# A two-layer transformer kernel without the constant products in TensorE's planned holes

## The reference, cut to what matters

```python
x = L0_attn_x                                     # (8, 1024, 256)
x = x + attn0(layernorm(x), w_qkv, w_out)         # 16 heads of 16, causal softmax
x = x + ffn0(layernorm(x), proj, C1, Win1, Wout1, C2, Win2, Wout2)
x = x + attn1(layernorm(x), Wq_down, ..., Wc)     # latent 64 per head, rotary half, causal
x = x + ffn1(layernorm(x), Ws1, Ws2, W1, W2, Wr)  # shared expert + top-2 of 8, prob truncated
# ffn0: a = entmax15(layernorm(x @ proj)); h = gelu(((x,1) @ Win1 * (a @ C1)) @ Wout1.T)
#       out = ((h,1) @ Win2 * (a @ C2)) @ Wout2.T
# ffn1: relu(x @ Ws1)**2 @ Ws2 + trunc(softmax(top2(x @ Wr))) * expert outputs
```

## Time and profile before

| | |
|---|---|
| runs, median (lowest to highest) | 2942.04 us (2939.97 to 2944.25) |
| the profiled execution's own time | 2941.76 us |
| its span, first to last instruction | 2940.0 us |
| mean granted TensorE clock | 0.975 of full |
| TensorE busy (its matmuls) | 2637.8 us, 90% |
| VectorE, ScalarE, GpSimd busy | 2091.0, 1895.6, 948.8 us |
| filler products, line 1119, busy (435 of 520 have a record) | 119.2 us |
| chain that ended last, by engine | PE 64%, ACT 13%, DVE 13%, issue 5% |

### The profile page before, as it was taken

The page is one execution under the profiler, slowest core; times in us unless marked ns, Lnnn a source line. Parts: engine busy times, 40 slices in busy tenths (PEclk is TensorE's granted clock), DMA queues, the critical chain, the costliest instruction groups (busy, mean ns, idle before and its releaser), DMA issues.

```text
span 2940.0 us, 56496 instructions
## 1 busy us (share of the span) xinstructions
PE 2637.8 (90%) x18768; PEld 1101.7 (37%) x18853; DVE 2091.0 (71%) x5808; ACT 1895.6 (64%) x3868; POOL 948.8 (32%) x1646
## 2 busy tenths in 40 slices
PE   6989998999889998999989999899988999889987
PEld 4334432334333443334433343333433334333432
DVE  4865687857868588685887668776687757878483
ACT  3565665767566766667666675576766776566655
POOL 2214241425214251243413234142521425114411
PEclk9999999999999999999999999999999999999999
DMA  5202120212102120121211112011210213101120
GB/s 185 55 1 60 44 55 18 68 47 80 37 27 64 57 80 18 32 75 45 75 26 42 56 58 69 19 58 42 77 49 24 62 46 89 31 25 46 32 59 16
DMA packets 138734, 150.43 MB, mean 51 GB/s; under 512 B 15920, under 2 KB 122832, under 8 KB 138448
## 3 DMA queue, kind: packets, MB, share of 16 engines
q1 hardware_dynamic: 138448, 146.74, 17.3%
HBM read 78.46 MB, written 67.11 MB: 50 GB/s over the span
## 4 chain that ended last, share of the span: by engine, by line
PE 64%; ACT 13%; DVE 13%; issue 5%; POOL 1%; DMA 1%; SPq 0%; ACTq 0%; DVEq 0%; POOLq 0%
PE ps L1254 15%; PE ps L1170 9%; ACT probs L1557 9%; PE ps L1235 7%; PE ps L1194 7%; PE ps L1162 6%; DVE mx L1824 4%; PE ps L1333 4%; PE ps L1328 4%; DVE ps L1821 4%; PE ps L1119 2%; PE ps L1320 2%; PE ps L1262 2%; PE ps L1208 1%; PE ps L1137 1%
## 5 line engine op out<-in xcount | busy, mean ns | idle before, releaser
L1557 ACT ACTIVATE probs<-ps 128x512 f32<-128x512 f32 (+2 forms) x2560 | 1235.0, 564 | 371.5 <-PE ps L1235 365.5
L1824 DVE TENSOR_REDUCE mx<-ps 128x1 f32<-128x512 f32 (+2 forms) x1536 | 900.3, 639 | 251.5 <-PE ps L1208 125.9
L1821 DVE CUSTOM_DVE_ANT_0 ps<-ps,mask_b 128x512 f32<-128x512 f32 (+1 forms) x1024 | 614.6, 650 | 251.4 <-PE ps L1194 249.6
L1729 POOL TENSOR_SCALAR_AFFINE_SELECT probs<-probs 128x256 f32<-128x256 f32 (+1 forms) x768 | 368.8, 484 | 1110.9 <-ACT probs L1557 1108.5
L1254 PE MATMUL ps<-probs,vaug 128*17 128x512 f32 (+3 forms) x6144 | 618.7, 513 | 8.7 <-ACT probs L1557 3.7
L1194 PE MATMUL ps<-stk_k,stk_q 48*128 48x512 f16 (+3 forms) x3072 | 458.3, 333 | 60.8 <-issue 36.6
L1235 PE MATMUL ps<-stk_q,stk_k 50*128 50x512 f16 (+3 forms) x3072 | 439.0, 333 | 63.5 <-ACT probs L1557 20.5
L1194 PEld LDWEIGHTS ps<-stk_k,stk_q 48*128 48x128 f16 x3072 | 138.1, 94 | 437.8 <-issue 347.3
L1235 PEld LDWEIGHTS ps<-stk_q,stk_k 50*128 50x128 f16 x3072 | 131.5, 94 | 440.8 <-issue 338.4
L1162 PE MATMUL ps<-turned,wqkv 128*128 128x512 f32 x512 | 262.0, 619 | 9.2 <-ACT scratch L1522 2.1
L1254 PEld LDWEIGHTS ps<-probs,vaug 128*17 128x17 f32 x6144 | 139.6, 98 | 295.9 <-issue 202.0
(11 more groups left out here) (171 smaller groups left out, 2902.0 us busy)
## 6 DMA issues: line engine op xcount, KB each, us to landing
stk_q<-q SPq DMA_DIRECT2D x256, 96.0 KB, 2.5
stk_k<-k SPq DMA_DIRECT2D x128, 192.0 KB, 3.6
q<-parts SPq DMA_DIRECT2D x64, 256.0 KB, 2.3
k<-parts SPq DMA_DIRECT2D x64, 256.0 KB, 2.2
stk_k<-k SPq DMA_DIRECT2D x128, 96.0 KB, 2.5
x<-in_L_attn_x SPq DMA_DIRECT2D x16, 512.0 KB, 4.0
q<-parts SPq DMA_DIRECT2D x64, 128.0 KB, 2.8
k<-parts SPq DMA_DIRECT2D x64, 128.0 KB, 2.1
```

Source lines behind the costliest of these rows:

```text
L1557: act.activation(probs[:, step % PBUF, heads, cols], src, ACT.Exp, scale=exponent[l])\
L1729: pool.affine_select(out=diag, in_=diag, compare_op=ALU.is_ge, fill=0.0, base=0, pattern=[[0, k], [1, P]], channel_multiplier=-1).then_inc ...
L1821: dve.tensor_tensor_reduce(tile, tile, mask_b[:, BANK - width:BANK], 1.0, LOWEST, ALU.add, ALU.max, most)\
L1824: dve.tensor_reduce(most, tile.rearrange("q (k w) -> q k w", k=k), AX.X, ALU.max)\
```

## The change

The products are no longer issued, and with them go the note in the planner, the two constants, the helper and its eight calls. The wait on `pool_chain` ahead of the first place goes too. `ORDER` stays as it is.

```diff
--- before.py
+++ after.py
@@ -649,9 +649,6 @@
         else:
             what()
         if what != "wait":
-            item = plan.order[made]
-            if gap > FILL_FROM and item[0] in ("xt", "yt", "at", "st", "mt", "s", "nm", "lg", "rt"):
-                FILL[item] = int(gap / FILL_TIME)
             gap = 0.0
 
     order = plan.order
@@ -682,8 +679,6 @@
 RANK = dict(mt=1, nm=2, burst=3, late=4, st=5, pair=5.5, due=6, s=7, chain=8, single=10)
 EARLY = True
 
-FILL_TIME, FILL_FROM = 0.25, 0.7
-FILL = {}
 
 PLACE = {}
 FINISH = []
@@ -1112,12 +1107,6 @@
                 return t_bank[b], full[b]
 
 
-            def keep_going(key, pt):
-                if FILL.get(key, 0) and key == next(iter(FILL)):
-                    pe.wait_ge(pool_chain, 9)
-                for _ in range(FILL.get(key, 0)):
-                    pe.matmul(pt, ident_b[:], mask_b[:], start=True, stop=True)
-
             def tile(key):
                 b = PLACE[key][0]
                 return t_bank[b], full[b]
@@ -1131,7 +1120,6 @@
 
             def transposed_x(n, b, c, kd):
                 pt, done = claim(("xt", n, b, c, kd))
-                keep_going(("xt", n, b, c, kd), pt)
                 pe.wait_ge(xn_ready, 2 * (LN["rstd", n, b, c] + 1))
                 for i in range(TPC):
                     ins = pe.transpose(pt[:, P * i:P * (i + 1)], xn[:, i, P * kd:P * (kd + 1)], ident[:])
@@ -1184,7 +1172,6 @@
                 c, slot = UNITS[u][3], u % NBUF
                 width = dict(score_parts(i))[p]
                 n, tiles = packed(width), [claim(("s", u, i, h, p, r)) for r in range(2)]
-                keep_going(("s", u, i, h, p), tiles[0][0])
                 pe.wait_ge(stk_loaded[slot], 16 * STACK_DMAS * (u // NBUF + 1))
                 for a in range(n):
                     for r in range(2):
@@ -1213,7 +1200,6 @@
 
             def max_rows(u):
                 pt, done = claim(("mt", u))
-                keep_going(("mt", u), pt)
                 rows = pt[0:2 * NP * PAIRS, 0:BANK // 2].bitcast(F16)
                 pe.wait_ge(mx_ready, u + 1)
                 for i in range(TPC):
@@ -1223,7 +1209,6 @@
             def scores_t(u, j, h):
                 c, slot = UNITS[u][3], u % NBUF
                 tiles = [claim(("st", u, j, h, r)) for r in range(2)]
-                keep_going(("st", u, j, h), tiles[0][0])
                 if j == 0 and h == 0:
                     pe.wait_ge(m_loaded, 16 * MAX_DMAS * (MT["mt", u] + 1))
                 a, z = query_range(j, c)
@@ -1264,7 +1249,6 @@
 
             def transposed_y(b, l, c, kd):
                 pt, done = claim(("yt", b, l, c, kd))
-                keep_going(("yt", b, l, c, kd), pt)
                 in_sbuf(pe, ("nm", LAST_UNIT[b, l, c]))
                 for i in range(TPC):
                     ins = pe.transpose(pt[:, P * i:P * (i + 1)], y[:, PASS[b, l, c] % 2, i, P * kd:P * (kd + 1)], ident[:])
@@ -1285,7 +1269,6 @@
 
             def narrow_product(key, n, b, c, w):
                 pt, done = claim(key)
-                keep_going(key, pt)
                 need_xT(n, b, c)
                 for kd in range(KD):
                     for t in range(TPC):
@@ -1300,7 +1283,6 @@
 
             def transposed_a(b, c):
                 pt, done = claim(("at", b, c))
-                keep_going(("at", b, c), pt)
                 pe.wait_ge(a_ready, ENT["epow", b, c] + 1)
                 for i in range(TPC):
                     ins = pe.transpose(pt[0:STRIP + E0, P * i:P * (i + 1)], zu[:, i, :], ident[:])
```

## The result

| | median | lowest to highest | runs |
|---|---|---|---|
| before | 2940.39 us | 2934.94 to 2950.33 | 18 |
| changed | 2948.9 us | 2940.61 to 2958.18 | 18 |

The account below looks back on a forecast made before the run. TensorE's fillers were taken to be partly on the path, standing behind bank waits and starving ScalarE. 2941.8 - 45 (path) + 25 (clock falls) + 6.5 (covered phases, tail, start) gave 2928 us, range 2898 to 2958 us.

Parts of the forecast that it names:

- The gain on the path (45 us): Time returned at the end by dropping fillers: at most 60 us from 278 on the path, taken as 45 us.
- the place of rows 4: Three fillers behind a bank's wait, ahead of a score product: ScalarE's idle 0.89 us would shrink to 0.24 us.
- rival B: TensorE would wait for VectorE, ScalarE or a DMA instead: 30 us gained, 25 + 6.5 lost, 2943 us; chance 0.18.
- The 90 places: Places of the 278 fillers taken to be on the path, each 0.216 us, 60 us in all if fully returned.
- 23 falls: New drops to the lower clock between 90 and 2780 us, 3.3 us long, 1.1 us lost each: 25 us.
- The sevens: Six runs of seven fillers ahead of `s` items, beside the maxima's DMAs: 42 fillers, removal gives 0.
- eight thin stretches a batch: 5 us stretches with TensorE too little busy once fillers go; three in eight lose the clock, 3 new falls a batch.
- the 33 places: Places of the 242 fillers taken to be covered by VectorE, a DMA or other waits: removal gives 0 path.
- the three covered phases: 68 to 90, 255 to 283, 2780 to 2829 us: clock falls almost surely, only the way back up costs, 3 us.
- the tail: Last transpositions and products after 27 fillers and 3 behind: no path gain, 3 us lost at the lower clock.
- Rival A: Holes between 90 and 2780 us stay thin, 45 falls at 1.3 us: +20 us, 2961 us; decides from 35 falls; chance 0.24.
- Rival C: Fillers never bought clock between 90 and 2780 us; only tail and edges are lost: 2903 us; chance 0.15.

Follow-up runs that it names:

- the first experiment: From the kernel before, keeps only the 242 fillers at 33 places taken as covered and drops the 278 at the other 90: 2917.67 us, ratio 0.9919.
- experiments 9 and 10: From the kernel before, 95 fillers ahead of `st` items dropped (9): 2927.74 us, 0.9951; 165 ahead of `s` items dropped (10): 2923.39 us, 0.9937.
- experiment 2: From the kernel before, keeps the 278 fillers at 90 places and drops the 242 at the 33 covered places: 2969.36 us, ratio 1.0091.
- experiment 5: The changed kernel with only the six runs of seven fillers (42, ahead of `s` items) put back: 2926.66 us, ratio 0.9956 to the kernel before.

## Why the prediction was wrong

**The gain on the path (45 us).** The mechanism was right: the place of rows 4 gives 0.67 us, the seven lay beside the DMA. Subtracting the starts of the same ScalarE instructions in the kernel before and in the first experiment's, the batch from 1392 to 1744 us has seven steps clear of a fall, of 0.25 to 0.79 us, together 4.4 us; others lie beside a difference in clock. The five batches of both have 89 us at the lower level, so that their 18.4 us are path alone: 3.7 a batch, where 5.9 were forecast. For the whole program, the 24 us of the first experiment and what its clock lost make 33 us by the profiled execution and up to 40 us by the runs' medians. 45 was too high; that of a filler's 0.216 us only 0.11 to 0.15 reach the end (experiments 9 and 10) is in line with rival B's mechanism, other waits that follow.

**The 90 places as a whole.** The prediction had 23 falls for all places between 90 and 2780 us. The sevens were one of its eight thin stretches a batch, at three in eight, so six of them were some 2 falls, and the 90 places had -45 + 21 x 1.1 = -22 us; the first experiment measured -24 us. Its clock says 6 falls more by the profiled execution and 13 by the runs' medians, not 21. The sum is right, and its two terms are each too large: that is luck. (The eight doesn't follow from the rule beside it either. Twelve places a batch, one a seven and half of the other eleven thin, are 6.5 stretches; that would have been 19 falls, 20 us and a forecast of 2923 us.)

**The step that failed: the price of the covered places.** For the 33 places at which removal gives no path, the prediction had some 2.5 us for the six sevens (2 falls), about one price each for the three covered phases (3 us), 3 us for the tail and 0.5 for the start: 9 us. They cost 31 us (2948.9 against 2917.67), and 28 us when they alone were dropped (experiment 2). The reasoning was that VectorE or a DMA covers what happens there, and that a hole brings down the clock for one fall or none. The first is so in the place itself: from 68.6 to 90.1 us the changed kernel ran at

```profile
68.60:90.10 21.50, 11.82 (x77) 5.42 (x76) 20.02 (x66) 3.62 (x7) 2.56 (x8) 0.63 0.08 24
```

and VectorE is as busy as in rows 7. But the lower level outlasts the hole and meets work that has no cover. Its longest stretch, in the place of unit 8's 34 fillers, has the length of seven falls, where one price was taken:

```profile
258.30:282.30 24.00, 12.47 (x77) 6.86 (x79) 17.09 (x74) 8.23 (x16) 8.04 (x12) 0.51 0.42 122
```

Six sevens cost 18 to 21 us instead of 2.5, since each brought two to three falls and not three eighths of one. The last 150 us cost 8.9 us (159.8 - 150.9) instead of about 4; in the other two kernels without these fillers they took 158.1 (experiment 2) and 153.9 us (experiment 5), so that this term is between 3 and 9 us.

**The clock.** I forecast 23 falls more between 90 and 2780 us, 76 us at the lower level, and some 40 us elsewhere. By the trace's record of the clock it was 107 us more between 90 and 2780 us (from 126 to 234), of which 24 in the stretch above, and 55 us elsewhere (from 10 to 26 us ahead of it, from 12 to 52 us behind). Without unit 8's stretch the 107 us are 83, or 24 falls: the number was right and the places weren't, more at the sevens and fewer at the 90. At the start, in unit 8 and at the end 79 us are twice the 40 forecast.

Rival A's outcome came in, the slower one, at +8 and not +20 us. Its place did so in part: 107 us are 31 falls, under its turning point of 35, and what tipped the sum were the sevens and the covered places, not the holes at the 90 places. The falls at the covered places were also cheaper than the others: experiment 2 had 0.020 less clock in the runs' median, some 119 us, and lost 28 us, 0.24 us a microsecond. Rival B names part of the gain that didn't come (30 us, against 33 to 40), but it held the edges to cost 6.5 us as the forecast did. Rival C is out, with the reading of the Trainium skill's rule on which it stood (TensorE: Matmul & The Clock Gate, section "Why this matters for your kernels"): without the fillers in the 90 places, whose planned holes are 0.7 to 1.8 us, the runs' median clock is 0.967 and not 0.975, and with those in six holes of some 2 us put back into the changed kernel it is 0.958 and not 0.947.

**The signs named beforehand.** ScalarE's wait closed as said (0.89 to 0.14); the DMA of `mT` is named; the first 90 us are no shorter. Two failed. A batch took 1754.0/5 = 350.8 us where 349 was forecast (1760.9/5 = 352.2 before, by the same stretch): the five have 38 us more at the lower level, 2.2 falls each where 3 were forecast, so that it is the gain that was too small. And the clock was 0.947 where 0.955 was, which the start, unit 8 and the end account for.

**What stays open.** Why one missing run of seven brings two to three falls. In the kernel of experiment 5 the falls just in front of the seven's place are missing as well, so one fall may bring others in the next batch; no run was made to separate that. Nor was a run made that drops the tail's fillers or those of unit 8 alone, so that what is left of the 31 us beside the sevens isn't divided among them.

## What to carry to other kernels

A filler behind the wait that makes its hole costs time, here 0.11 to 0.15 us of its 0.216, and one in front of that wait little or none. So what has to be asked of a filler is which semaphore it stands behind: moving the 520 between the waits for an item's two banks is worth 48 us (58 us with 788 of them), while removing them is worth nothing. Before removing work that is hidden, price what the clock does after the cover ends, not in the hole. And a chain of waits that names such work is to be checked against the item behind it: it booked 5.8 us on the tail's fillers, and without them the item behind comes no earlier: from the start of the projection to the transposition it was 9.46 us with them (2912.18 to 2921.64) and 9.56 us without them in experiment 5, where the projection ran at full clock.

## What the runs showed of the hardware

A product of one row and one column with 512 moving columns took 373 ns against 379 ns for 128x128 cells, yet the program with 520 of them ran at a mean clock of 0.937, below the 0.947 of the one with none. Six holes of some 2 us, one in a batch, filled or empty, are 0.958 or 0.947 of clock. And one program's mean clock isn't fixed: the changed kernel's 18 runs lie between 0.942 and 0.951, and its time follows over 18 us, so that one profile of such a kernel is one draw.
